# Stack ends: variance, mean and gates at other places in their engines' orders; entry: v weights and chunk 1 rounded between q and k

## The chip, the cores and the metric

The kernel runs on one core of a Trainium2 chip. That core has TensorE (PE, matrix products; PEld is its weight load), VectorE (DVE), ScalarE (ACT), GpSimd (POOL) and SyncE (SP, which issues the DMAs). Every engine works through its own list of instructions in the order in which they were written, and the engines meet only through semaphores. The metric is the device time of one execution in microseconds. The kernel before took 3382.31 us (median of 3 runs, 3380.04 to 3384.08).

## The reference

The input is 2048 tokens of width 128. Two stacks (the same weights, different input) stand around a Mamba block:

```python
x = x + 0.5 * ffn_ref(layernorm(x))        # stack 0: DEPTH = 6 layers
x = x + mamba_ref(layernorm(x))
x = x + 0.5 * ffn_ref(layernorm(x))        # stack 1: the same six layers

for i in range(6):                         # inside ffn_ref
    x = attn_layer(shift_tokens(x), ...) + x   # q,k,v = x @ Wqkv, l2norm, rotary,
                                               # windows of 32 keys, softmax, @ Wo
    x = ffn_layer(shift_tokens(x), ...) + x    # layernorm (mean, variance), W1, a*gelu(gate), W2
```

## The kernel before, in words

The tokens lie along the free axis, 16 tiles of 128 tokens per layer, 96 tiles per stack. A tile goes through a software pipeline whose steps `s` are counted up to 114: at every step each engine does its own piece of tiles of different age, in the order in which the step functions are called in `tensor_stack`, `scalar_stack`, `vector_stack` and `pool_stack`. There is no scheduler: the order written in these functions is the order on the engines.

**Entry of a stack.** The input is normalised in four chunks of 512 tokens (`square_in`, `rsqrt_in`, `scale_in`). Products of q, k and v are made from a high and a low part: ACT rounds weights (`high_weights`, L805) and input chunks (`high_input`, L794) to the high part, POOL subtracts to get the low part (`low_weights`, L1544; `low_input`, L1535). After `q_project(0)` and `k_project(0)` the first tile's chain is: ACT squares q and k (`q_square` L832, `k_square` L839), DVE rotates (`q_rotate1` L1190, `q_rotate2` L1199, `k_rotate1` L1208, `k_rotate2` L1214), sums squares (L1226, L1232) and floors the sums (`floor_sums`, L1238), POOL adds the halves (`q_add_halves` L1562, `k_add_halves` L1568) and multiplies with the inverse norms (`q_normalise` L1576, `k_normalise` L1584; the inverse norms are ACT L850). q's and k's second rotated halves share one buffer, T2, so `q_rotate2(1)` waits until POOL has done `k_add_halves(0)`, and `k_project(1)` on PE waits for `q_rotate2(1)`. In stack 1 POOL also clears PTS (`memset` L1623), which `p_evacuate(0)` on ACT needs later.

**End of a stack.** The feed-forward part works on units of four tiles. The last four tiles are two units of 256 columns, which the code calls `u + 1` (tiles 92 and 93) and `u + 2` (tiles 94 and 95), with `u` the last unit of 512. The end is written out by hand (`finish_tiles` on PE, the code behind the step loop on the others). A unit goes: mean product (`centre_product`, L427), square (ACT L932), variance product (L447), inverse root (`inverse_root`, ACT L942 and L944), normalise (DVE L1284, L1286), high part (ACT L957), low part (POOL L1596), up products (L468 to L470, 18 matmuls), gelu (ACT L971), gate (DVE L1308, three), down products (`down_products`, L521, three matmuls, which the trace shows as six), and `half_output` (DVE L1329, L1331), which adds the result to X. `residual(95)` on DVE (L1270, L1271) must be done before the mean product of `u + 2`, and it follows `out_products(95)` on PE (L404), which follows `o_evacuate(95)` on ACT (L922) and `value_products(95)` on PE (L384). The Mamba block starts when the last `half_output` is done; at the end of stack 1 the same event lets SP send the last piece of the output.

Of the kernel before, what the change touches and what calls it, by code (L numbers as in the profile page):

```python
# [31 lines left out]
def build(nc, xT, consts, wqkv, wo, w1, w2, lpar, qks, mpar, in_w, xp_w, dt_w, out_w, out):  # L32
    ctx = ExitStack()
    with ctx:
# [61 lines left out]
        PTS = take(2048)  # L96
# [95 lines left out]
        def tensor_stack(pe, r):  # L192
# [352 lines left out]
            def finish_tiles():  # L545
# [6 lines left out]
                u = UNITS - 3  # L552
# [42 lines left out]
                centre_product(u + 1, 4)  # L595
                tile(oT_ev, 94)
                out_products(94, 2)
                tile(PT_ev, 95)
                pe.wait_ge(v2_in[1], 160 * ((n0 + 95) // 2 + 1))
                value_products(95)  # L600
                units(f_sq, u + 1)
                variance_product(u + 1, 5)
                tile(oT_ev, 95)
                tile(res_done, 94)
                out_products(95, 2)
                units(f_lo, u + 1)
                up_products(u + 1, 0, 0)
                up_products(u + 1, 1, 1)
                units(f_done, u)
                up_products(u + 1, 2, 3)  # L610
                tile(res_done, 95)
                units(f_xm, u + 1)
                centre_product(u + 2, 4)
                units(f_sq, u + 2)
                units(f_ln, u + 1)
                variance_product(u + 2, 5)
# [150 lines left out]
        def scalar_stack(act, r):  # L767
# [66 lines left out]
            def k_square(n):  # L834
                if not 0 <= n < N:
                    return
                act.wait_ge(k_done, n0 + n + 1)
                act.wait_ge(q_ss, n0 + n + 1)
                act.activation(SQ, PS[:, 0, :], ACT.Square).then_inc(k_sq, 1)  # L839
# [166 lines left out]
            for s in range(114):  # L1006
                if s == 17 + 1:
                    square_in(3)
                    high_weights(0, 2)
                    high_input(1)  # L1010
                if s == 17 + 2:
                    rsqrt_in(3)
                    high_input(2)
                    if r == 0:
                        act.wait_ge(const_in, 48)
                if s == 19 + 2:
                    split_up(0)
                if s == 19 + 4:
                    high_input(3)
                ffn_high(s - 23)  # L1020
                split_k(s - 18)
                exponentials(s - 20)
                q_evacuate(s - 19)
                o_evacuate(s - 21)
                k_evacuate(s - 19)
                gelu0(s - 23)
                gelu1(s - 23)
                gelu2(s - 23)
                q_square(s - 17)
                v_evacuate(s - 19)  # L1030
                restore_tables(s - 23)
                inverse_norms(s - 18)
                carry_evacuate(s - 18)
                split_input(s - 24)
                ffn_square(s - 22)
                ffn_rsqrt(s - 22)
                p_evacuate(s - 20)
                k_square(s - 17)
                split_v(s - 19)
                split_q(s - 17)  # L1040
# [13 lines left out]
            p_evacuate(95, 0)  # L1054
            tables(act)
            square(u + 1, 4)
            o_evacuate(95)
            inverse_root(u + 1, 5)
            high_part(u + 1)
            square(u + 2, 4)  # L1060
            inverse_root(u + 2, 5)
# [101 lines left out]
        def vector_stack(dve, r):  # L1163
# [257 lines left out]
            gate(u + 1, 0, 0)  # L1421
            gate(u + 1, 1, 1)
            gate(u + 1, 2, 3)
            half_output(u + 1, 5)
            gate(u + 2, 0, 6)
            gate(u + 2, 1, 7)
            gate(u + 2, 2, 2)
            half_output(u + 2, 4)

        def vector_mamba(dve):  # L1430
# [98 lines left out]
        def pool_stack(pool, r):  # L1529
# [85 lines left out]
            for s in range(113):  # L1615
                if s == 17 + 1:
                    low_weights(0, 2)
                    low_input(1)
                if s == 17 + 2:
                    low_input(2)  # L1620
                    if r == 1:
                        pool.wait_ge(m_out, 4)
                        nc.gpsimd.memset(PTS, 0.0).then_inc(zero_set, 1)  # L1623
                if s == 17 + 8:
                    low_input(3)
                ffn_low(s - 23)
# [254 lines left out]
```

## Time and profile before

| | us |
|---|---|
| median of 3 runs | 3382.31 |
| lowest, highest | 3380.04, 3384.08 |
| the profiled execution | 3384.22 |
| its span, first to last instruction | 3382.3 |
| PE busy | 3193.0 (94%) |
| DVE busy | 2792.2 (83%) |
| ACT busy | 2509.8 (74%) |
| POOL busy | 2434.0 (72%) |
| mean granted TensorE clock | 0.984 |

The profiled execution took 1.9 us more than its span. Stack 0 runs from the start to 1548.85 us, the Mamba block from there to about 1835 us, and stack 1 to the end. In the slices of the page PE is at 9 tenths in nearly all of both stacks, and lower in the first slice and in the Mamba block, so the change touches four short stretches at whose edges PE isn't full: two entries and two ends.

### The profile page before, as it was taken

How to read it: one execution, taken by the hardware profiler on the slowest of the kernel's cores; microseconds unless marked ns; L12 is line 12 of the kernel's file. 1: busy time of each engine (PE TensorE's matmuls, PEld its weight loads, DVE VectorE, ACT ScalarE, POOL GpSimd, SP SyncE). 2: the span in 40 equal slices, each digit the busy share in tenths (PEclk: the TensorE clock that was granted, in tenths of full speed). 3: DMA queues.
4: the chain of work that ended last, by engine and by line, in shares of the span. 5: the costliest groups of instructions: out<-in, count | busy, mean ns of one | idle time of the engine just before them, and what ended most of it. 6: DMA issues, size and time to landing. Idle time of an engine off the chain costs nothing.

```text
span 3382.3 us, 120360 instructions
## 1 busy us (share of the span) xinstructions
PE 3193.0 (94%) x51584; PEld 2524.8 (75%) x51584; DVE 2792.2 (83%) x3200; ACT 2509.8 (74%) x3167; POOL 2434.0 (72%) x1227
## 2 busy tenths in 40 slices
PE   7999999999999999997788899999999999999998
PEld 5888887887888887773223788888878788888776
DVE  6888888888888888875897888888888888888885
ACT  5777777777787777776675677777777777777775
POOL 6777776776777777750998777777768768768663
PEclk9999999999999999998899899999999999999999
DMA  3333233233333332221000332323323323323222
GB/s 112 89 76 89 69 89 84 69 85 83 77 78 91 73 83 66 72 70 37 10 1 0 83 77 69 91 69 82 91 67 87 90 70 79 94 64 90 64 65 64
DMA packets 142298, 245.21 MB, mean 72 GB/s; under 512 B 32397, under 2 KB 34638, under 8 KB 141774
## 3 DMA queue, kind: packets, MB, share of 16 engines
q1 hardware_dynamic: 141774, 237.51, 27.6%
q8 instruction: 415, 6.80, 0.8%
q14 instruction: 109, 0.89, 0.1%
HBM read 35.01 MB, written 1.05 MB: 11 GB/s over the span
## 4 chain that ended last, share of the span: by engine, by line
PE 78%; DVE 7%; issue 7%; POOL 4%; ACT 4%; DMA 0%; DVEq 0%; SPq 0%; POOLq 0%; ACTq 0%
PE PS L264 14%; PE PS L384 11%; PE PS L208 8%; PE PS L404 8%; PE PS L210 7%; PE PS L209 7%; PE PS L325 6%; PE PS L521 4%; ACT ARENA L860 3%; PE PS L468 2%; PE PS L470 2%; PE PS L469 2%; POOL ARENA L1672 2%; PE PS L427 1%; DVE ARENA L1496 1%
## 5 line engine op out<-in xcount | busy, mean ns | idle before, releaser
L1576 POOL TENSOR_TENSOR ARENA<-ARENA,RN 128x1024 f32<-128x1024 f32 x192 | 365.4, 1903 | 454.9 <-ACT RN L850 454.9
L264 PE MATMUL PS<-C,ARENA 128*128 128x128 f32 x4608 | 613.9, 276 | 33.3 <-ACT ARENA L860 16.3
L1568 POOL TENSOR_TENSOR ARENA<-ARENA 128x1024 f32<-128x1024 f32 x192 | 468.4, 2439 | 232.9 <-DVE ARENA L1214 231.9
L264 PEld LDWEIGHTS PS<-C,ARENA 128*128 128x128 f32 x4608 | 512.3, 141 | 110.2 <-issue 76.9
L208 PE MATMUL PS<-WL,XH 128*128 128x512 f32 x1152 | 490.1, 425 | 19.1 <-DVE ARENA L1214 7.4
L913 ACT ACTIVATE ARENA<-PS 64x1024 f32<-64x1024 f32 x384 | 390.2, 1016 | 98.5 <-PE PS L264 95.0
L1562 POOL TENSOR_TENSOR ARENA<-ARENA 128x1024 f32<-128x1024 f32 x192 | 457.4, 2382 | 4.2 <-DVE ARENA L1199 4.2
L210 PE MATMUL PS<-WH,XH 128*128 128x512 f32 x1152 | 455.9, 396 | 0.0
L209 PE MATMUL PS<-WH,XL 128*128 128x512 f32 x1152 | 454.3, 394 | 0.0
L384 PE MATMUL PS<-ARENA 128*64 128x64 f32 x12288 | 403.2, 224 | 41.8 <-DVE ARENA L1252 26.0
L384 PEld LDWEIGHTS PS<-ARENA 128*64 128x64 f32 x12288 | 378.3, 139 | 76.5 <-issue 76.3
L1190 DVE TENSOR_TENSOR ARENA<-PS,TAB 128x1024 f32<-128x1024 f32 x192 | 235.1, 1225 | 229.9 <-ACT ARENA L832 229.8
L1590 POOL TENSOR_TENSOR ARENA<-ARENA,RI 128x1024 f32<-128x1024 f32 x192 | 365.8, 1905 | 47.7 <-DVE RI L1263 41.4
L404 PEld LDWEIGHTS PS<-ARENA 128*128 128x128 f32 x3072 | 372.1, 191 | 18.0 <-ACT ARENA L922 1.8
L1584 POOL TENSOR_TENSOR ARENA<-ARENA,RN 128x1024 f32<-128x1024 f32 x192 | 374.5, 1950 | 1.5 <-ACT RN L850 1.5
L404 PE MATMUL PS<-ARENA 128*128 128x128 f32 x3072 | 373.9, 275 | 1.0 <-ACT ARENA L922 1.0
L325 PEld LDWEIGHTS PS<-ARENA 64*32 64x32 f32 x24576 | 292.4, 105 | 69.5 <-issue 59.2
L325 PE MATMUL PS<-ARENA 64*32 64x64 f32 x24576 | 326.0, 223 | 0.3 <-issue 0.3
L1244 DVE TENSOR_REDUCE MX<-PS 128x16 f32<-128x1024 f32 x192 | 234.5, 1222 | 94.6 <-PE PS L325 91.7
L922 ACT ACTIVATE ARENA<-PS 128x1024 f32<-128x1024 f32 x192 | 196.9, 1026 | 143.4 <-PE PS L384 143.4
L208 PEld LDWEIGHTS PS<-WL,XH 128*128 128x128 f32 x1152 | 218.5, 190 | 77.1 <-issue 17.6
L832 ACT ACTIVATE ARENA<-PS 128x1024 f32<-128x1024 f32 x192 | 197.1, 1027 | 98.4 <-PE PS L210 98.4
(147 smaller groups left out, 6487.7 us busy)
## 6 DMA issues: line engine op xcount, KB each, us to landing
ARENA<-ARENA SPq DMA_DIRECT2D x1152, 128.0 KB
ARENA<-ARENA SPq DMA_DIRECT2D x768, 64.0 KB
ARENA<-in_wqkv SPq DMA_DIRECT2D x36, 512.0 KB, 5.1
ARENA<-in_wo SPq DMA_DIRECT2D x12, 512.0 KB, 4.0
ARENA<-in_w SPq DMA_DIRECT2D x12, 341.0 KB, 3.6
ARENA<-in_w SPq DMA_DIRECT2D x12, 192.0 KB, 4.1
X<-in_xT SPq DMA_DIRECT2D x4, 256.0 KB, 5.7
out<-X SPq DMA_DIRECT2D x1, 768.0 KB, 3.4
```

Source lines behind the costliest of these rows:

```text
L208: nc.tensor.matmul(o, XH[:, x], WL[:, s], start=True, stop=False)
L209: nc.tensor.matmul(o, XL[:, x], WH[:, s], start=False, stop=False)
L210: last = nc.tensor.matmul(o, XH[:, x], WH[:, s], start=False, stop=True)
L264: last = nc.tensor.transpose(PS[:, slot, 128 * j:128 * j + 128], src[:, 128 * j:128 * j + 128], ident)
L325: last = nc.tensor.matmul(PS[32 * win:32 * win + 32, slot, c:c + 64], q[a:b, hp, 32 * win:32 * win + 32], kt[a:b, hp, 32 * win:32 * win + ...
L384: last = nc.tensor.matmul(out.rearrange("p (a q) -> p a q", a=2)[:, :, col:col + 32], v2[:, win, hp, :], pt[:, hp, win, :], start=True, st ...
L404: last = nc.tensor.matmul(PSB[:, bank, 0:128], w[:, 128 * j:128 * j + 128], OTS[:, 128 * j:128 * j + 128], start=j == 0, stop=j == 7)
L913: last = act.activation(blocks[a:b, :, par, :], PS[a:b, slot, :].rearrange("p (b q) -> p b q", q=32), ACT.Copy)
L1562: nc.gpsimd.tensor_tensor(QN[n % 2], QN[n % 2], T2, ALU.add).then_inc(q_add, 1)
L1568: nc.gpsimd.tensor_tensor(KN[n % 2], KN[n % 2], T2, ALU.add).then_inc(k_add, 1)
L1584: nc.gpsimd.tensor_tensor(a, a, bc(RN[:, n % 2, 16:32], 64), ALU.mult).then_inc(k_nrm, 1)
L1590: nc.gpsimd.tensor_tensor(heads(P), heads(P), bc(RI[:, n % 2, :], 64), ALU.mult).then_inc(p_nrm, 1)
```

## The change

No instruction is added or taken away. These move:

- PE, both stack ends: the variance product of `u + 1` goes ahead of `value_products(95)`; the mean product of `u + 2` goes up between the first and the second of the three up products of `u + 1`.
- ACT, both stack ends: `inverse_root(u + 1)` goes ahead of `o_evacuate(95)`.
- DVE, both stack ends: `half_output(u + 1)` goes behind the three gates of `u + 2`.
- ACT, both entries: the high parts of the v weights and of input chunk 1 go from behind `square_in(3)` to ahead of `k_square(0)`.
- POOL, both entries: `low_input(2)` goes from step 19 to step 22, and in stack 1 the clearing of PTS from step 19 to step 20.

```diff
@@ finish_tiles (PE)
                 out_products(94, 2)
+                units(f_sq, u + 1)
+                variance_product(u + 1, 5)
                 tile(PT_ev, 95)
                 pe.wait_ge(v2_in[1], 160 * ((n0 + 95) // 2 + 1))
                 value_products(95)
-                units(f_sq, u + 1)
-                variance_product(u + 1, 5)
                 tile(oT_ev, 95)
                 tile(res_done, 94)
                 out_products(95, 2)
                 units(f_lo, u + 1)
                 up_products(u + 1, 0, 0)
+                tile(res_done, 95)
+                units(f_xm, u + 1)
+                centre_product(u + 2, 4)
                 up_products(u + 1, 1, 1)
                 units(f_done, u)
                 up_products(u + 1, 2, 3)
-                tile(res_done, 95)
-                units(f_xm, u + 1)
-                centre_product(u + 2, 4)
@@ k_square (ACT)
+                if n == 0:
+                    high_weights(0, 2)
+                    high_input(1)
@@ scalar_stack
                 if s == 17 + 1:
                     square_in(3)
-                    high_weights(0, 2)
-                    high_input(1)
@@
             square(u + 1, 4)
+            inverse_root(u + 1, 5)
             o_evacuate(95)
-            inverse_root(u + 1, 5)
@@ vector_stack
-            half_output(u + 1, 5)
             gate(u + 2, 0, 6)
             gate(u + 2, 1, 7)
             gate(u + 2, 2, 2)
+            half_output(u + 1, 5)
             half_output(u + 2, 4)
@@ pool_stack
-                if s == 17 + 2:
+                if s == 17 + 3 and r == 1:
+                    pool.wait_ge(m_out, 4)
+                    nc.gpsimd.memset(PTS, 0.0).then_inc(zero_set, 1)
+                if s == 17 + 5:
                     low_input(2)
-                    if r == 1:
-                        pool.wait_ge(m_out, 4)
-                        nc.gpsimd.memset(PTS, 0.0).then_inc(zero_set, 1)
```

The end of a stack on PE, as the difference of the two orders: L404 is `out_products`, L384 `value_products(95)`, L447 the variance product of `u + 1`, L427 a mean product.

```order
 L427 MATMUL PS<-ARENA,C 128x256
 L404 MATMUL PS<-ARENA 128x128 x8
-L384 MATMUL PS<-ARENA 64x2x32 x32
 L447 MATMUL PS<-ARENA,C 128x256
+L384 MATMUL PS<-ARENA 64x2x32 x32
 L404 MATMUL PS<-ARENA 128x128 x8
 L468 MATMUL PS<-XNH,W1L 128x256
```

The variance product is now one place further ahead, in front of the 32 value products. The mean product of `u + 2` moves up by twelve matmuls in the same way (the diff above shows it).

The end of stack 1 on DVE before: L1308 are the gates (three a unit), L1329 and L1331 the two halves of `half_output`.

```order
L1308 SCALAR_TENSOR_TENSOR ARENA<-PS,LP,ARENA 128x256 x2
L1308 SCALAR_TENSOR_TENSOR ARENA<-PS,LP,ARENA 85x256
L1329 SCALAR_TENSOR_TENSOR X<-PS,LP,X 64x256
L1331 SCALAR_TENSOR_TENSOR X<-PS,LP,X 64x256
L1308 SCALAR_TENSOR_TENSOR ARENA<-PS,LP,ARENA 128x256 x2
L1308 SCALAR_TENSOR_TENSOR ARENA<-PS,LP,ARENA 85x256
L1329 SCALAR_TENSOR_TENSOR X<-PS,LP,X 64x256
L1331 SCALAR_TENSOR_TENSOR X<-PS,LP,X 64x256
```

And now (in the changed kernel these lines have numbers that are higher by one):

```order
L1309 SCALAR_TENSOR_TENSOR ARENA<-PS,LP,ARENA 128x256 x2
L1309 SCALAR_TENSOR_TENSOR ARENA<-PS,LP,ARENA 85x256
L1309 SCALAR_TENSOR_TENSOR ARENA<-PS,LP,ARENA 128x256 x2
L1309 SCALAR_TENSOR_TENSOR ARENA<-PS,LP,ARENA 85x256
L1330 SCALAR_TENSOR_TENSOR X<-PS,LP,X 64x256
L1332 SCALAR_TENSOR_TENSOR X<-PS,LP,X 64x256
L1330 SCALAR_TENSOR_TENSOR X<-PS,LP,X 64x256
L1332 SCALAR_TENSOR_TENSOR X<-PS,LP,X 64x256
```

All six gates now stand ahead of both half outputs.

The entry of stack 1 on POOL before, from `low_input(1)` on: L1535 makes low parts of input chunks, L1568 is `k_add_halves`, L1576 `q_normalise`, L1562 `q_add_halves`, L1584 `k_normalise`, L1623 clears PTS, and in the piece after it L1591 (before L1590) is `p_normalise(0)`.

```order
L1535 TENSOR_TENSOR XL<-ARENA,XH 128x512
L1568 TENSOR_TENSOR ARENA<-ARENA 128x1024
L1576 TENSOR_TENSOR ARENA<-ARENA,RN 128x1024
L1562 TENSOR_TENSOR ARENA<-ARENA 128x1024
L1584 TENSOR_TENSOR ARENA<-ARENA,RN 128x1024
L1535 TENSOR_TENSOR XL<-ARENA,XH 128x512
L1623 MEMSET ARENA 128x2048
L1568 TENSOR_TENSOR ARENA<-ARENA 128x1024
L1576 TENSOR_TENSOR ARENA<-ARENA,RN 128x1024
L1562 TENSOR_TENSOR ARENA<-ARENA 128x1024
L1584 TENSOR_TENSOR ARENA<-ARENA,RN 128x1024
L1568 TENSOR_TENSOR ARENA<-ARENA 128x1024
```

And now:

```order
L1536 TENSOR_TENSOR XL<-ARENA,XH 128x512
L1569 TENSOR_TENSOR ARENA<-ARENA 128x1024
L1577 TENSOR_TENSOR ARENA<-ARENA,RN 128x1024
L1563 TENSOR_TENSOR ARENA<-ARENA 128x1024
L1585 TENSOR_TENSOR ARENA<-ARENA,RN 128x1024
L1569 TENSOR_TENSOR ARENA<-ARENA 128x1024
L1577 TENSOR_TENSOR ARENA<-ARENA,RN 128x1024
L1563 TENSOR_TENSOR ARENA<-ARENA 128x1024
L1585 TENSOR_TENSOR ARENA<-ARENA,RN 128x1024
L1622 MEMSET ARENA 128x2048
L1569 TENSOR_TENSOR ARENA<-ARENA 128x1024
L1591 TENSOR_TENSOR ARENA<-ARENA,RI 128x1024
```

`low_input(2)` is gone from this place (it now stands ahead of `k_add_halves(4)`), and the clearing of PTS now stands ahead of `k_add_halves(2)` and `p_normalise(0)`. The row ahead of this piece, the low part of the v weights, keeps its place on POOL, but ACT's part before it comes earlier.

## Rows read from the trace of the kernel before

**Rows 1.** The page's chain that ended last, share of the span by engine.

```profile
PE 78%; DVE 7%; issue 7%; POOL 4%; ACT 4%; DMA 0%; DVEq 0%; SPq 0%; POOLq 0%; ACTq 0%
```

**Rows 2.** Stretches: from:to us, length, busy of each engine, granted clock, DMA share, GB/s.

```profile
20.00:30.00 10.00, 7.87 (x25) 5.03 (x24) 7.23 (x9) 4.27 (x6) 3.92 (x3) 0.84 0.02 7
...
200.00:1480.00 1280.00, 1250.79 (x21810) 1032.29 (x21806) 1083.69 (x1246) 982.74 (x1212) 942.67 (x466) 1.00 0.31 78
...
1536.00:1542.00 6.00, 5.71 (x22) 5.35 (x23) 1.26 (x3) 4.32 (x8) 0.24 (x1) 0.50 0.00 0
```

**Rows 3.** Timeline, PE, end of stack 0: start, length, instruction, [idle before <-releaser].

```profile
1522.96 2.08 PE L384 MATMUL PS<-ARENA 128*64 128x64 f32 x64
...
1526.16 2.05 PE L404 MATMUL PS<-ARENA 128*128 128x128 f32 x16 [0.49 <-ACT ARENA L922]
1529.14 0.39 PE L468 MATMUL PS<-XNH,W1L 128*128 128x256 f32 x1 [0.92 <-POOL XNL L1596]
...
1532.42 0.70 PE L447 MATMUL PS<-ARENA,C 128*128 128x256 f32 x2 [0.47 <-ACT ARENA L932]
1536.29 0.58 PE L468 MATMUL PS<-XNH,W1L 128*128 128x256 f32 x1 [3.17 <-POOL XNL L1596]
...
1540.30 2.40 PE L521 MATMUL PS<-ARENA 128*128 128x256 f32 x6
1545.27 2.57 PE L521 MATMUL PS<-ARENA 128*128 128x256 f32 x6 [2.57 <-DVE ARENA L1308]
```

**Rows 4.** Timeline, ACT, end of stack 0.

```profile
1527.87 0.42 ACT L957 ACTIVATE XNH<-ARENA 128x256 fp32r<-128x256 f32 x1 [0.94 <-DVE ARENA L1286]
...
1540.54 0.47 ACT L971 ACTIVATE ARENA<-PS,LP 85x256 f32<-85x256 f32 x1 [0.81 <-PE PS L470]
```

**Rows 5.** Timeline, DVE, end of stack 0.

```profile
1528.55 0.29 DVE L1271 TENSOR_TENSOR ARENA<-PS,ARENA 64x128 f32<-64x128 f32 x1
...
1543.75 1.26 DVE L1308 SCALAR_TENSOR_TENSOR ARENA<-PS,LP,ARENA 128x256 f32<-128x256 f32 x3
```

**Rows 6.** Timeline, PE and DVE, end of stack 1.

```profile
3371.74 1.47 PE L521 MATMUL PS<-ARENA 128*128 128x256 f32 x6
...
3378.72 0.47 DVE L1329 SCALAR_TENSOR_TENSOR X<-PS,LP,X 64x256 f32<-64x256 f32 x1 [3.19 <-PE PS L521]
3379.20 0.49 DVE L1331 SCALAR_TENSOR_TENSOR X<-PS,LP,X 64x256 f32<-64x256 f32 x1
```

**Rows 7.** Timeline, DVE, PE and ACT, entry of stack 0.

```profile
33.66 1.23 DVE L1190 TENSOR_TENSOR ARENA<-PS,TAB 128x1024 f32<-128x1024 f32 x1 [0.57 <-ACT ARENA L832]
...
35.40 1.23 DVE L1199 TENSOR_TENSOR ARENA<-PS,TAB 128x1024 f32<-128x1024 f32 x1 [0.52 <-POOL ARENA L1568]
...
36.88 0.47 PE L208 MATMUL PS<-WL,XH 128*128 128x512 f32 x1 [1.30 <-DVE ARENA L1199]
...
38.55 1.02 ACT L839 ACTIVATE ARENA<-PS 128x1024 f32<-128x1024 f32 x1 [4.18 <-PE PS L210]
```

**Rows 8.** Timeline, all engines, entry of stack 1.

```profile
1857.30 2.00 POOL L1544 TENSOR_TENSOR WL<-ARENA,WH 128x1024 fp32r<-128x1024 f32 x1 [4.55 <-ACT WH L805]
...
1858.99 1.22 DVE L1190 TENSOR_TENSOR ARENA<-PS,TAB 128x1024 f32<-128x1024 f32 x1 [2.06 <-ACT ARENA L832]
...
1862.86 1.23 DVE L1199 TENSOR_TENSOR ARENA<-PS,TAB 128x1024 f32<-128x1024 f32 x1 [2.65 <-POOL ARENA L1568]
...
1864.34 0.76 PE L208 MATMUL PS<-WL,XH 128*128 128x512 f32 x1 [3.43 <-DVE ARENA L1199]
...
1867.28 1.02 ACT L839 ACTIVATE ARENA<-PS 128x1024 f32<-128x1024 f32 x1 [7.58 <-PE PS L210]
...
1884.72 2.37 POOL L1568 TENSOR_TENSOR ARENA<-ARENA 128x1024 f32<-128x1024 f32 x1
...
1892.42 1.06 PE L264 MATMUL PS<-C,ARENA 128*128 128x128 f32 x8 [0.16 <-issue]
```

**Rows 9.** One line's instructions, L1238: shortest/median/longest in ns.

```profile
L1238 DVE TENSOR_SCALAR SS<-SS x192: 115/118/2144, 31.8 to 3321.2; 128x32 f32<-128x32 f32 x192
```

## The prediction

> **What bounds the kernel now.** I read the chain that ended last first: 78% of the span is PE's [rows 1]. The table of stretches then says that in the loop PE is busy 1250.79 of 1280 us [rows 2], so nothing is to be had or lost there unless an order of the loop changes, and none does. What the change touches are the edges, so I read the timelines of the two entries and the two ends, engine by engine, and looked at the idle time in brackets. At the end of stack 0 PE waits 0.49 us for ACT, 0.92 for POOL, 0.47 for ACT, 3.17 for POOL and, between the two down products, 2.57 for the gates on DVE [rows 3]. At the entry of stack 1, DVE waits 2.65 us for POOL's `k_add_halves(0)` and PE 3.43 us behind it; at the entry of stack 0 the same two waits are 0.52 and 1.30 [rows 7, 8]. An edge is a single chain: each us taken out of its longest path moves everything after it, because what follows waits for it.
>
> **End of a stack, the gates.** Before, DVE stands in `half_output(u + 1)` until PE has done the down products of `u + 1`, and only then makes the three gates of `u + 2` (1543.75 to 1545.01 us) [rows 5], though the last gelu of `u + 2` was done at 1541.01 [rows 4]. PE's second down product waits for these gates [rows 3]. Now the gates come first: the last one starts at 1541.05 and takes about 0.42 (a third of 1.26), so it is done at 1541.5, while PE is in the first down product until 1542.70. The second follows at about 1542.6 instead of 1545.27: 2.7 us less. `half_output(u + 1)` now runs beside the second down product; nothing waits for it but X, and at the end of stack 1 its small output transfer. In stack 1 the first down product ran at the higher clock (1.47 us, 3371.74 to 3373.21) [rows 6]. With no gap the second should too: 3373.21 + 1.4 + 0.04 + the 0.97 us of `half_output` = 3375.6 instead of 3379.69 [rows 6], 4.1 us less. Bounds: if it takes 2.57 us as in stack 0, 2.9 us less; if stack 0's pair ran at the higher clock, 1.1 (2.57 - 1.47) to 2.0 us more there.
>
> **End of a stack, variance and mean.** In times of stack 0. The variance product of `u + 1` starts at 1522.96 ahead of the value products [rows 3] and pushes them by about 0.43 us (0.70 long, its tail lies under the next). So `out_products(95)` starts at 1526.6 instead of 1526.16: this is the price, since ACT's `o_evacuate(95)`, for which it waits, comes that much later. What it buys: ACT's inverse root and DVE's normalise now lie beside the value products. The high part, before at 1527.87 [rows 4], goes right behind `o_evacuate(95)` at about 1526.5, and POOL's low part (0.72 us) is done at 1527.7, before `out_products(95)` ends at 1528.6. The 0.92 us wait ahead of the up products is gone, and they start at 1528.45 instead of 1529.14. Then the mean product of `u + 2` stands behind the first third of them and needs `residual(95)`: `out_products(95)` ends at 1528.64, the residual takes 0.6 us (before it ended at 1528.84) [rows 5], so PE waits some 0.15 us. The 18 matmuls and the mean product took from 1529.14 to 1531.95 (1532.42 less the 0.47 idle) [rows 3], 2.81 us. ACT's square now lies beside the other twelve, so the 0.47 wait goes. New start of the last variance product: 1528.45 + 0.15 + 2.81 = 1531.4, less 0.1 for a shorter tail, 1531.3: 1.1 us less. The 3.17 us chain behind it (root, normalise, high, low) stays as it is. The bounds: 0 if the residual comes so late that PE waits out the gain (0.7 + 0.47 us), 1.3 if no wait is left. I take 1.1, for both stacks.
>
> **Entry of stack 1.** ACT is idle ahead of `k_square(0)`, so rounding the v weights (1.05 us) and chunk 1 (0.62) there costs nothing; ACT's next input, k's product, comes later. POOL then makes the low v weights right after `q_add_halves(0)`, near 1852.8 instead of 1857.30 [rows 8], and `k_add_halves(0)` starts near 1856 and ends near 1858.3. `q_rotate2(1)` no longer waits for it: it follows `q_rotate1(1)` [rows 8], and its 2.65 us of idle time go. What is late next is PE's own square of q, at which `q_rotate1(1)` already waits. So `k_project(1)` starts 2.65 us earlier, after an idle time of 0.8 us instead of 3.43. In stack 0 it ran after 1.30 us idle with 0.47 us for its first matmul, in stack 1 with 0.76; to the next square it took 1.67 us there (36.88 to 38.55) and 2.94 here (1864.34 to 1867.28) [rows 7, 8]. That is the two clocks, and I expect the higher one here now: another 1.27. Together 3.9 us. If the clock stays low it is 2.65.
>
> **Entry of stack 0.** The same wait is 0.52 us there [rows 7], so 0.5 less. The v weights must have landed by 23 us instead of 28.7: the DMA engines are at 0.02 from 20 to 30 us [rows 2], so they had.
>
> **What POOL moves elsewhere.** `low_input(2)` (1.3 us) goes ahead of `k_add_halves(4)`, where POOL is idle for about a us; its user is the q product of tile 8. Nothing. The clearing of PTS (1.8 us) goes ahead of `k_add_halves(2)`, which stands at 1884.72 with no idle time before it [rows 8], so it does delay that and `p_normalise(0)` by 1.8 us. The latter ended at 1888.95, and PE's transpose of it started at 1892.42 behind other work [rows 8]: 3.4 us of cover, so nothing. If that cover were gone it would cost up to 1.8 us.
>
> **A rule that could speak against it.** L1238, VectorE's floor of the sums, takes 118 ns in the median and 2144 at most [rows 9]; the long ones end when a POOL instruction beside them ends. The Trainium skill (SBUF — State Buffer, "Who interferes with whom") says why: VectorE in a two-port mode and GpSimd share a port pair, and the later one fully blocks. By that rule the earlier `k_add_halves(0)` now stands beside the floor in both entries and holds it to about 33.6 and 1858.3 us. Without the rule the floor ends 1.7 or 1.4 us earlier, at 31.9 and 1856.9. The next rotation starts at 33.66 and 1858.99 [rows 7, 8] either way, but in stack 0 the margin is 0.1 us, so the 0.5 there is the weakest term. I keep it and put the loss into a rival.
>
> **The sum.** 0.5 + (2.7 + 1.1) + 3.9 + (4.1 + 1.1) = 13.4 us. The profiled execution took 3384.2, which gives 3370.8; the median of the runs is 1.9 lower, which gives 3368.9, or 3369.
>
> **The rivals.**
>
> *The stack ends give the reordering back, and the clock stays low at stack 1's entry* (0.15). For it: `out_products(95)` is later and the mean product now waits on a later residual; the clock there was low once [rows 8]. Against: the waits of 0.92 and 0.47 us do go. It costs 2 x 1.1 + 1.3 = 3.5 us: 3372.5.
>
> *The clock does better* (0.12). In stack 0's end the rows show 0.50 from 1536 to 1542 us although PE was busy 5.71 of 6 us [rows 2]; down products took 2.40 and 2.57 [rows 3] against 1.47 in stack 1 [rows 6]. With the gap of 2.57 gone, both could run at the higher clock, as could the first products of the Mamba block: 0.9 + 1.1 + about 1.5: 3365.5. The Trainium skill (TensorE: Matmul & The Clock Gate, Part 1) has the clock released by activity and low without it; by that, continuous work favours this case. The stretch at 0.50 with PE nearly full speaks against taking it as the forecast.
>
> *POOL's moved work shows* (0.07). The clearing of PTS and the blocked floor decide: 1.8 + 0.5 us: 3371.3.
>
> *Only the ends count* (0.05). The loop that follows swallows what the entries gain, because something other than this chain (a transfer, POOL) sets when PE is full. Against: from tile 4 on PE has almost no idle time, so an earlier start stays. 4.4 us back: 3373.3.
>
> *The loop settles at a longer pitch* (0.03, the slower side). Engines wait for each other in a circle, and an entry with other offsets could leave one more short wait in each step. PE's 0.16 us wait ahead of a transpose shows the kind [rows 8]; one more of it in each of 192 tiles is 31 us, less 13: 3400. It decides from 13.4 / 192 = 0.07 us a tile on. Against: the order in the loop is the same, and both stacks, with different entries, take the same time for the loop within about 2 us.
>
> *Most of it doesn't work* (0.03): another wait stands at once behind each one removed, and less than half of the sum is left: 3377.
>
> The forecast has 0.55. Its own spread from the clock (1.3 us a term) and from runs that differ by 2 us is 3365.5 to 3372.5. The range that should hold 8 in 10 reaches up to the first rival and half of the fourth and down to the second: 3364 to 3374.5. What a measurement can tell here is about 0.2%, 6.8 us, so faster means under 3375.5: 0.92. Within it 0.05; slower 0.03.
>
> **What the profile after would show.** No wait of DVE for L1568 in either entry, and `k_project(1)` in stack 1 after an idle time of about 0.8 us, with matmuls of 0.4 us. In the ends: no idle time between the two down products, the six gates behind each other, the last variance product 1.1 us closer to `out_products(94)`. The loop between as long as before. The prediction is wrong if `q_rotate2(1)` still waits for POOL, if PE idles over 0.5 us ahead of the moved mean product, or if the stretch from tile 8 to tile 90 has another length.

## The result, and the profile after

The changed kernel took 3362.34 us (median of 4 runs, 3360.05 to 3367.87), the kernel before 3382.48 us beside it (4 runs). The ratio is 0.9943 with a 95% interval of 0.9926 to 0.9961: 20.1 us less, where 13.4 were forecast. The time lies below the range given. The profiled execution took 3364.21 us with a span of 3362.4, 20.0 us less than the profiled execution before (3384.22).

The end of stack 0 on PE, timeline of the changed kernel (start, length, instruction, idle time before it), answers to [rows 3]:

```profile
1523.44 1.95 PE L404 MATMUL PS<-ARENA 128*128 128x128 f32 x16
1525.22 0.60 PE L447 MATMUL PS<-ARENA,C 128*128 128x256 f32 x2
...
1528.96 2.05 PE L404 MATMUL PS<-ARENA 128*128 128x128 f32 x16 [1.12 <-ACT ARENA L925]
1530.77 0.37 PE L468 MATMUL PS<-XNH,W1L 128*128 128x256 f32 x1
...
1531.70 0.70 PE L427 MATMUL PS<-ARENA,C 128*128 128x256 f32 x2
...
1533.67 0.59 PE L447 MATMUL PS<-ARENA,C 128*128 128x256 f32 x2
1537.43 0.58 PE L468 MATMUL PS<-XNH,W1L 128*128 128x256 f32 x1 [3.17 <-POOL XNL L1597]
...
1541.16 2.97 PE L521 MATMUL PS<-ARENA 128*128 128x256 f32 x12
1545.20 3.70 PE L683 MATMUL PS<-X,C 128*128 128x512 f32 x8 [1.07 <-DVE X L1332]
```

The up products follow `out_products(95)` without idle time, the last variance product follows the up products without idle time, and the two pairs of down products are one group of 12 that takes 2.97 us; before they were 2.40, a gap of 2.57, and 2.57 [rows 3]. The same pieces before, not among the rows above, with the first products of the Mamba block as the last:

```profile
1521.08 1.95 PE L404 MATMUL PS<-ARENA 128*128 128x128 f32 x16
...
1548.91 5.44 PE L683 MATMUL PS<-X,C 128*128 128x512 f32 x8 [1.07 <-DVE X L1331]
```

The same eight products take 3.70 us now and took 5.44 then. The new order of the gates explains the gap that went. It can't explain this: the products are the same and nothing stands between them, so it is the clock. The stretches (from:to, length, busy of PE, PEld, DVE, ACT, POOL, granted clock, DMA share, GB/s) say so, first of before, then of after:

```profile
1545.00:1553.00 8.00, 6.66 (x12) 3.38 (x13) 4.18 (x8) 0.93 (x2) 0.00 (x0) 0.57 0.22 72
1863.00:1878.00 15.00, 11.64 (x123) 9.07 (x127) 11.52 (x10) 6.50 (x8) 11.22 (x6) 0.66 0.00 0
```

```profile
1538.00:1544.00 6.00, 6.00 (x30) 5.17 (x28) 3.65 (x8) 3.79 (x7) 0.00 (x0) 0.77 0.01 4
1541.00:1549.00 8.00, 6.93 (x24) 3.99 (x23) 6.01 (x11) 3.61 (x6) 0.00 (x0) 1.00 0.25 74
1851.00:1864.00 13.00, 9.04 (x103) 6.92 (x105) 10.59 (x10) 6.81 (x10) 8.54 (x4) 1.00 0.00 0
...
200.00:1480.00 1280.00, 1250.67 (x21855) 1032.59 (x21856) 1083.74 (x1248) 983.31 (x1211) 942.15 (x466) 1.00 0.31 78
```

Around the last down products the clock was 0.50 [rows 2] and is 0.77; at the start of the Mamba block it was 0.57 and is 1.00; at the entry of stack 1, 0.66 and 1.00. The loop is what it was: PE busy 1250.67 of 1280 us, against 1250.79. Summed over the span, the granted clock was at its lower level (1.2 of 2.4 GHz) for 106 us before and for 78 after (an expectation below has 108, which counts 2 us behind the last instruction).

DVE at the end of stack 0, and at the end of stack 1 with PE's down products, timelines of the changed kernel, answer to [rows 5, 6]:

```profile
1541.86 0.48 DVE L1309 SCALAR_TENSOR_TENSOR ARENA<-PS,LP,ARENA 85x256 f32<-85x256 f32 x1 [0.47 <-ACT ARENA L974]
1542.65 0.48 DVE L1330 SCALAR_TENSOR_TENSOR X<-PS,LP,X 64x256 f32<-64x256 f32 x1 [0.31 <-PE PS L521]
...
1544.17 0.48 DVE L1330 SCALAR_TENSOR_TENSOR X<-PS,LP,X 64x256 f32<-64x256 f32 x1 [0.53 <-PE PS L521]
```

```profile
3355.21 3.49 PE L521 MATMUL PS<-ARENA 128*128 128x256 f32 x12
...
3359.23 0.49 DVE L1332 SCALAR_TENSOR_TENSOR X<-PS,LP,X 64x256 f32<-64x256 f32 x1
```

The last gate now follows its gelu, and the half outputs wait for PE only. In stack 1, 4.5 us lie between the start of the down products and the end (3355.21 to 3359.72), against 7.95 before (3371.74 to 3379.69 [rows 6]).

The entry of stack 1, timeline of the changed kernel, DVE, PE, ACT and POOL, answers to [rows 8]:

```profile
1848.66 1.53 DVE L1239 TENSOR_SCALAR SS<-SS 128x32 f32<-128x32 f32 x1
...
1852.03 1.21 DVE L1200 TENSOR_TENSOR ARENA<-PS,TAB 128x1024 f32<-128x1024 f32 x1
```

```profile
1853.49 0.47 PE L208 MATMUL PS<-WL,XH 128*128 128x512 f32 x1 [0.69 <-DVE ARENA L1200]
...
1860.36 0.47 PE L208 MATMUL PS<-WL,XH 128*128 128x512 f32 x1 [1.65 <-DVE ARENA L1215]
...
1877.71 1.06 PE L264 MATMUL PS<-C,ARENA 128*128 128x128 f32 x8 [0.16 <-issue]
```

```profile
1855.15 1.02 ACT L842 ACTIVATE ARENA<-PS 128x1024 f32<-128x1024 f32 x1 [3.56 <-PE PS L210]
...
1844.59 1.99 POOL L1545 TENSOR_TENSOR WL<-ARENA,WH 128x1024 fp32r<-128x1024 f32 x1
...
1847.78 2.38 POOL L1569 TENSOR_TENSOR ARENA<-ARENA 128x1024 f32<-128x1024 f32 x1
```

`q_rotate2(1)` (L1200) waits for nobody, and `k_project(1)` comes after 0.69 us of idle time, not 3.43 [rows 8], with a first matmul of 0.47 us, not 0.76. The entry of stack 0, DVE and PE, answers to [rows 7]:

```profile
33.35 1.23 DVE L1191 TENSOR_TENSOR ARENA<-PS,TAB 128x1024 f32<-128x1024 f32 x1 [0.18 <-ACT ARENA L832]
34.49 1.21 DVE L1200 TENSOR_TENSOR ARENA<-PS,TAB 128x1024 f32<-128x1024 f32 x1
```

```profile
36.60 0.58 PE L208 MATMUL PS<-WL,XH 128*128 128x512 f32 x1
...
43.76 0.76 PE L208 MATMUL PS<-WL,XH 128*128 128x512 f32 x1 [2.58 <-DVE ARENA L1215]
```

DVE's wait of 0.52 us went here too. But `q_project(2)`, at 43.76, stands behind 2.58 us of idle time, and it and the first v product run at the lower clock through all their twelve matmuls: from tile 3 on stack 0 is 1.9 us *later* than before in this profile.

Set one beside the other, start by start, the two traces give this account. "Waits" is what the idle time that went brought to the next piece, "clock" is the same instructions taking another time.

| stretch | forecast | trace | waits | clock |
|---|---|---|---|---|
| entry of stack 0 | 0.5 | -1.9 | 0 | -1.9 |
| loop of stack 0 | 0 | -0.5 | | |
| end of stack 0 | 3.8 | 6.1 | 3.8 | 2.3 |
| Mamba block | 0 | 4.4 | 0 | 4.4 |
| entry of stack 1 | 3.9 | 6.0 | 2.7 | 3.3 |
| loop of stack 1 | 0 | 0.6 | | |
| end of stack 1 | 5.2 | 5.3 | 3.8 | 1.5 |
| sum | 13.4 | 20.0 | 10.3 | 9.6 |

The forecast of 13.4 had some clock in it already: 1.27 us in the entry of stack 1 and about 1.5 at the end of stack 1.

### The profile page after: what moved, and what is told of

Same layout as the page of the kernel before. It is cut to its first block, busy times and chain, and to the rows that moved or that the text cites. A ratio compares the mean times of both kernels' runs of the same rounds, so it can differ in the third digit from the quotient of the medians.

```text
span 3362.4 us, 120360 instructions
## 1 busy us (share of the span) xinstructions
PE 3178.5 (95%) x51584; PEld 2519.0 (75%) x51584; DVE 2793.3 (83%) x3200; ACT 2511.4 (75%) x3167; POOL 2434.8 (72%) x1227
## 4 chain that ended last, share of the span: by engine, by line
PE 77%; DVE 7%; issue 7%; POOL 5%; ACT 4%; DMA 0%; DVEq 0%; SPq 0%; POOLq 0%; ACTq 0%
PE PS L264 14%; PE PS L384 11%; PE PS L208 8%; PE PS L404 8%; PE PS L210 7%; PE PS L209 7%; PE PS L325 6%; PE PS L521 4%; ACT ARENA L863 3%; PE PS L468 2%; PE PS L470 2%; PE PS L469 2%; POOL ARENA L1673 2%; PE PS L427 1%; DVE ARENA L1497 1%
## 5 line engine op out<-in xcount | busy, mean ns | idle before, releaser
L384 PE MATMUL PS<-ARENA 128*64 128x64 f32 x12288 | 404.5, 225 | 41.7 <-DVE ARENA L1253 25.8
L384 PEld LDWEIGHTS PS<-ARENA 128*64 128x64 f32 x12288 | 379.5, 139 | 76.8 <-issue 76.8
L1591 POOL TENSOR_TENSOR ARENA<-ARENA,RI 128x1024 f32<-128x1024 f32 x192 | 366.0, 1906 | 47.2 <-DVE RI L1264 37.1
L404 PEld LDWEIGHTS PS<-ARENA 128*128 128x128 f32 x3072 | 372.1, 191 | 18.6 <-ACT ARENA L925 2.5
L404 PE MATMUL PS<-ARENA 128*128 128x128 f32 x3072 | 373.8, 275 | 2.2 <-ACT ARENA L925 2.2
```

What stands on the lines that cost most here:

```text
L384: last = nc.tensor.matmul(out.rearrange("p (a q) -> p a q", a=2)[:, :, col:col + 32], v2[:, win, hp, :], pt[:, hp, win, :], start=True, st ...
L404: last = nc.tensor.matmul(PSB[:, bank, 0:128], w[:, 128 * j:128 * j + 128], OTS[:, 128 * j:128 * j + 128], start=j == 0, stop=j == 7)
L1591: nc.gpsimd.tensor_tensor(heads(P), heads(P), bc(RI[:, n % 2, :], 64), ALU.mult).then_inc(p_nrm, 1)
```

## The experiments

The theory (T): the waits went as forecast, some 10.5 us in all, and the rest is TensorE's clock, which stays up where PE no longer stops. The rival (S): some part has a structural gain of its own that the forecast overlooked. A median of 11 runs has an interval of about 3 us on either side, one of 5 runs about 4 to 5, so no two results closer than that are told apart by the medians alone. The kernel before took 3382.3 to 3383.7 us beside these kernels.

### The parts, each alone

**Gates.** The kernel before with DVE's change alone (as in the diff of the change, `vector_stack`).

> The kernel before with the gates of the last unit ahead of half_output of the unit before it, in both ends, and nothing else. Theory T (the moves gain what their waits cost, and the rest of the gain of 20 us is TensorE's clock, which is granted at its low level for fewer us): 2.7 us in stack 0 and 4.1 in stack 1 by the waits, 6.8, and some us more where the last products and the first ones of the Mamba block get the high clock: 7 to 10 us less than before, and no stretch at the low clock behind the last up products longer than 3.4 us. Rival S (a structural gain was overlooked in one of the parts, the clock differs by chance): exactly one of the three part kernels gains 6 us more than its waits say; here that would be 13.

3374.98 us, ratio 0.9977 (0.9968 to 0.9986): 8.7 less. The timeline of PE at the end of stack 0 in this kernel:

```profile
1541.55 3.48 PE L521 MATMUL PS<-ARENA 128*128 128x256 f32 x12
1546.11 3.70 PE L683 MATMUL PS<-X,C 128*128 128x512 f32 x8 [1.07 <-DVE X L1331]
```

The gates alone join the down products and bring the Mamba block's first products to the higher clock (3.70 us). They are worth 4.0 us in stack 0's end by the trace, 2.57 of it the gap (the pair itself took 3.48 us instead of 4.97), and 1.7 in the first products behind it, which the Mamba block gave back later in this profile.

**Variance and mean.** The changes of `finish_tiles` on PE and of `inverse_root` on ACT alone.

> The kernel before with the variance product, the mean product and ACT's inverse root moved in both ends, and nothing else. Theory T: 1.1 us in each end, 2.2 less, plus or minus 2 by the clock. Rival S: 8 less. Rival G (the reorder is given back by the later out products): no gain.

3377.86 us, ratio 0.9984 (0.9975 to 0.9993): 5.8 less, against 2.2 forecast. That is outside T's 2.2 plus or minus 2 and under S's 8, and with an interval of 3 us it decides between neither. In its profile each end's waits give 1.2 to 1.3 us, as worked out; another 2.4 in the end of stack 0 and 1.4 in that of stack 1 come from matmuls that ran at the higher clock. The down products at the end of stack 0 in this kernel:

```profile
1540.26 1.47 PE L521 MATMUL PS<-ARENA 128*128 128x256 f32 x6
1544.30 1.54 PE L521 MATMUL PS<-ARENA 128*128 128x256 f32 x6 [2.57 <-DVE ARENA L1308]
```

The idle times of 3.17 and 2.57 us stand here as before, and still these products took 1.47 and 1.54 us, not 2.40 and 2.57 [rows 3]. So an idle time doesn't always slow the same work behind it. In the six profiles whose end of stack 1 is that of the kernel before (before, e_entry, entry_act_only, entry_pool_only, s0_entry, s1_entry) the stretch from the last variance product to the end took from 16.8 to 19.1 us with the same idle times. What holds in every profile is the first eight products of the Mamba block: 3.70 us in the nine profiles where the gap of 2.57 is gone or filled, 5.18 to 6.56 us in the seven where PE idles in it.

**Entry.** ACT's and POOL's changes of both entries.

> The kernel before with the entry's moves on ACT and POOL in both stacks, and nothing else. Theory T: 0.5 us in stack 0 and 2.65 in stack 1 by the waits, and 1.3 to 3 by the clock in stack 1: 4.5 to 6 less than before; in stack 0 the profile can show up to 2 us more than before, where the low clock falls on the products of tiles 2 and 3. Rival S: 10 less.

3374.92 us, ratio 0.9981 (0.9973 to 0.9990): 8.7 less, against 4.4 forecast; T had 4.5 to 6 and S 10, and the median is nearer to S. Its profile has 5.5 us in stack 1's entry.

**The whole again**, on the same chip as these three.

> The changed kernel once more, on the chip of its parts. Theory T: 20 us less than before, in single runs from 14 to 24, and the time falls with the total of us at the low clock (78 us in the first profile, 108 in the one of before); the parts' gains add to less than the whole, or to it, since each frees the clock for the next. If the parts add to 13.4 and the whole is 20, the parts act together, by the clock. Rival S: the parts add to 20 on this chip with equal clock totals.

3361.24 us (5 runs), ratio 0.9936 (0.9923 to 0.9950): 22.4 less. The three parts add up to 23.2. So no gain from their working together is to be seen, and each part alone gave 2 to 4 us more than its forecast (1.9, 3.6 and 4.3 us). No one part holds the 6 to 7 us by which the whole beat its forecast. Each of these three surpluses is near the interval of its median, so that none of them alone shows a cause.

### The entry taken apart, and the ends together

```
e_entry split by stack:  if n == 0 and r == 1 (s1_entry)   if n == 0 and r == 0 (s0_entry)
e_entry split by engine: ACT's rounding (entry_act_only)   POOL's two moves (entry_pool_only)
ends_both:               gates + variance and mean, entries as before
```

> The kernel before with ACT's part of the entry moved alone: POOL keeps the low part of chunk 2 and the clearing of PTS ahead of the second tile's k addition. Theory T: these two stand where POOL has idle time in stack 0; in stack 1 the clearing delays the second k addition by up to 1 us, beside other work: the same gain as the whole entry (8.7 us) within 1 us. Rival P (POOL's moves carry part of the gain): 3 us or more of it is missing.

> Kernel before with ACT's and POOL's entry changes in stack 1 alone. T (the waits go as predicted, and fewer stops of PE let its clock stay up): nearly all of the entry's gain is here, since the wait was 2.65 us in stack 1 and 0.52 in stack 0: 6.5 to 8.5 us less than before (the whole entry change gave 8.7), of which 2.65 to 4 from the waits and the rest by the clock at the products behind them. S (a structural gain that I overlooked, in stack 0's entry): at most 5 us less here.

> Kernel before with ACT's and POOL's entry changes in stack 0 alone. T: 0 to 2 us less than before, since the wait that goes is 0.52 us. S (the overlooked gain is in stack 0's entry): 3 us less or more.

> Kernel before with POOL's part of the entry change alone (the low part of chunk 2 and the clearing of PTS later; ACT's rounding stays where it was, so the v weights' low part still stands ahead of k's halves). T: the wait of 2.65 us stays, and the only gain is that of the work taken away ahead of k_add_halves(1) and its kin, the same 2.3 us by which the whole entry change beats ACT's part alone: 1 to 3 us less. P (POOL's part matters for the time of the whole in its own right, as a chain that was late by the 1.8 us of the clearing): 3 us less or more. N (it does nothing, and the 2.3 us between the two were noise): within 1 us.

> Kernel before with the changes of the ends alone: gates, variance and mean, both stacks. T: the two parts add up, 8.7 + 5.8 = 14.5, so 13 to 16 us less. C (the clock's share is one common pool, which each part takes for itself when it is alone): 10 to 12 us less, since the waits of the ends are 7.7 by the working and the clock's share (some 8 us in the whole) is then counted once.

| kernel | median us (runs) | ratio, 95% | less than before |
|---|---|---|---|
| entry_act_only | 3377.23 (11) | 0.9981 (0.9972 to 0.9990) | 6.4 |
| s1_entry | 3377.57 (11) | 0.9982 (0.9973 to 0.9991) | 5.4 |
| s0_entry | 3381.24 (11) | 0.9995 (0.9986 to 1.0004) | 1.7 |
| entry_pool_only | 3383.66 (11) | 1.0000 (0.9991 to 1.0009) | -0.7 |
| ends_both | 3369.50 (5) | 0.9959 (0.9945 to 0.9973) | 13.4 |

Most of the gain of the entry is that of ACT's rounding in stack 1. POOL's moves do nothing by themselves: entry_pool_only is rival N's case, and T's 1 to 3 us did not come. entry_act_only missed T too (the same gain within 1 us), by 2.3 us, which P's 3 us or more doesn't cover either. On these 2.3 us stood my expectation for entry_pool_only; they were noise or need ACT's part, and the medians don't tell. The profiles speak for noise of the clock: in entry_act_only the four idle products that the kernel before has itself ahead of `k_project(0)` (`keep_clock`, L215) took 3.78 us in stack 1, in e_entry 1.99. s0_entry's 1.7 lies in T's 0 to 2, within its interval of nothing. s1_entry missed T's 6.5 to 8.5 by a us and is above S's bound of 5; with an interval of 3 us it decides nothing by its median. Its profile does: from tile 0 to tile 6 of stack 1 it gains 6.6 us where the waits are 2.7. The ends add up within the intervals (13.4 against 8.7 + 5.8), where a pool of clock shared by the parts would have given 10 to 12.

### The clock by itself: fillers

If the surplus is the clock's, it must be had without moving any real work, by giving PE idle products to do where it waits. These are matmuls into a bank that is free there, whose result nobody reads. The kernel before has some of the kind itself, ahead of `k_project(0)`, `q_project(1)` and `k_project(1)` (`keep_clock`); these are added:

```diff
+            def fill(k, bank):
+                for _ in range(k):
+                    nc.tensor.matmul(PSB[:, bank, 0:256], centre, C[:, 0:256], start=True, stop=True)
@@ finish_tiles: ahead of the last up products, and (before only) between the down products
+                fill(11, 6)
                 units(f_lo, u + 2)
                 up_products(u + 2, 0, 6)
...
+                fill(9, 0)
                 for j in range(3):
                     units(f_h[j], u + 2)
@@ entries: 4 and 10 such products ahead of the transposes of k of tiles 0 and 1, 4 ahead of q_project(2);
@@ in stack 1, before only: 10 ahead of k_project(1)
```

> The kernel before with extra products into free PSUM banks, whose results nobody reads, where PE idles: 11 ahead of the last unit's up products and 9 between the down products (both ends), 4 ahead of the first k transpose, 10 ahead of the second, 4 ahead of the third q product, and 10 ahead of the second k product of stack 1. No order of the real work is changed. Theory T (part of the change's gain is the clock): with the clock held, up and down products of the ends and the first Mamba products run at the high level: 8 us less than before. Rival S (waits alone): the same time as before, or some us more where a filler stands in the way.

> The changed kernel with the same extra products (without the 9 between the down products and the 10 ahead of the second k product, where it has no idle time left). Theory T: 3 to 5 us less than the changed kernel; and the distance to the filled kernel before is what the waits alone give, about 15 us, against 22 unfilled. Rival S: the distance stays 22.

> The changed kernel with the 11 extra products ahead of the last unit's up products in both ends alone. Theory T: 2 to 3 us less than the changed kernel: the up products of the last unit at the high clock (2.2 us for 18 instead of 3 to 4). Rival S: no gain.

before_filled took 3377.18 us (11 runs), 6.5 less than before; full_filled 3362.84 and full_filled_ends 3360.64 (5 runs each), against 3361.24 for the changed kernel (measured on another chip; the kernel before took 3383.65 and 3383.63 us on the two). The distance between the filled kernels is 14.3 us, near T's 15 and not S's 22. But T's 3 to 5 us, and 2 to 3 for the ends alone, did not come, before_filled had 6.5 of T's 8, and the waits give 10.3 and not 14.3. The profile shows why. PE in before_filled, end of stack 0:

```profile
1537.61 0.47 PE L482 MATMUL PS<-XNH,W1L 128*128 128x256 f32 x1
...
1539.91 1.46 PE L535 MATMUL PS<-ARENA 128*128 128x256 f32 x6
1541.20 4.05 PE L219 MATMUL PS<-C 128*128 128x256 f32 x18
1545.09 1.46 PE L535 MATMUL PS<-ARENA 128*128 128x256 f32 x6
```

The down products (L535) run at the higher clock, 1.46 us against 2.40 and 2.57 [rows 3]. But the fillers (L219; one of them shows as two) take 4.05 us where 2.57 were idle, so that 3.7 us lie between the down products, and there is no idle time ahead of the real products behind them: the fillers ended last, and took back what they gave. So I sized them to the idle time: 7, 5 (before only), and 5 in the place of each 10.

```diff
-                fill(11, 6)
+                fill(7, 6)
...
-                fill(9, 0)
+                fill(5, 0)
```

> Kernel before with fillers of a fitting length: 7 idle products ahead of the last up products of each stack end (3.2 us by the 4.91 us that 11 took in before_filled, for an idle time of 3.17), 5 between the two down products (2.2 us for 2.57), and 5 in place of 10 in the entries. No wait of the real work is changed, only what PE does in it. In before_filled PE had no idle time ahead of these products and the fillers ended last, so part of what the clock gave was taken back. T (the part of the gain that the waits don't explain, 9 to 12 us, is the clock's, and comes when PE merely keeps busy): 8 to 12 us less than before, against 6.5 with the longer fillers. S (the rest is structural, in the order of real work): not more than the 6.5 again, or less.

> The changed kernel with the same shorter fillers (7 ahead of the last up products, 4/5/4 in the entries). T: 1 to 3 us less than the changed kernel (3361.2), and 10 to 12 us less than before_filled_less, the sum of the waits that the change took out by the trace (3.8 + 2.8 + 3.8 = 10.4), as the clock is up in both. S: the distance between the two filled kernels stays 14 us or more.

| kernel | median us (runs) | ratio, 95% | less than before | time at the lower clock |
|---|---|---|---|---|
| before_filled | 3377.18 (11) | 0.9980 (0.9971 to 0.9989) | 6.5 | 77 |
| before_filled_less | 3370.68 (6) | 0.9967 (0.9955 to 0.9979) | 11.6 | 52 |
| full_filled | 3362.84 (5) | 0.9936 (0.9923 to 0.9948) | 20.8 | 52 |
| full_filled_ends | 3360.64 (5) | 0.9931 (0.9919 to 0.9944) | 23.0 | 65 |
| full_filled_less | 3356.81 (5) | 0.9930 (0.9917 to 0.9942) | 25.5 | 65 |

The last column is of the profiled run, in us. before_filled_less is the run that decides: the kernel before, in its old order, with idle products in PE's waits, is 11.6 us faster (by the interval of the ratio 7 to 15); S had at most 6.5 there. The step from the longer fillers, 5 us, is within the intervals by the medians; the two traces show it: from the last variance product to the end of the stack it is 15.1 and 17.7 us with the longer fillers, 13.1 and 15.7 with the shorter, in stack 0 and 1 (16.5 and 18.2 without any). PE at the end of stack 0 in before_filled_less:

```profile
1536.09 1.53 PE L535 MATMUL PS<-ARENA 128*128 128x256 f32 x6
1537.46 2.32 PE L219 MATMUL PS<-C 128*128 128x256 f32 x10
1540.20 1.53 PE L535 MATMUL PS<-ARENA 128*128 128x256 f32 x6 [0.41 <-DVE ARENA L1324]
1542.81 3.70 PE L699 MATMUL PS<-X,C 128*128 128x512 f32 x8 [1.07 <-DVE X L1347]
```

Between the starts of the two down products lie 4.1 us, with the gates still behind `half_output(u + 1)`; before they were 4.97 [rows 3]. The end of the first and the start of the second are 2.57 us apart, as before. The Mamba block's first products take 3.70 us. The stretch that was at 0.50 before [rows 2]:

```profile
1536.00:1542.00 6.00, 5.23 (x22) 4.01 (x22) 2.46 (x6) 1.75 (x2) 0.00 (x0) 1.00 0.01 1
```

full_filled_less has the lowest median of the study, 4.4 us below that of the changed kernel, where T had 1 to 3; the ratios of the two (0.9930 and 0.9936) overlap, so the medians don't show that it is faster. It stands 13.9 us from before_filled_less, T having 10 to 12 and S 14 or more: between the two, it speaks for neither. Piece by piece the two traces stand 4.1 (end of stack 0), 1.7 (entry of stack 1) and 4.0 us (end of stack 1) apart, 9.8 together, near the 10.4 of T's working; the rest of the 13.9 lies within the intervals of two ratios of 6 and 5 runs. PE in full_filled_less, end of stack 0:

```profile
1530.76 3.18 PE L219 MATMUL PS<-C 128*128 128x256 f32 x14
1534.10 0.39 PE L480 MATMUL PS<-XNH,W1L 128*128 128x256 f32 x1
...
1536.58 2.83 PE L533 MATMUL PS<-ARENA 128*128 128x256 f32 x12
```

The up products start 3.77 us after the variance product (1530.33), as in the changed kernel (1533.67 to 1537.43), and take 2.5 us where they took 3.7. From the last variance product to the end it is 1.4 us less than in the changed kernel at the end of stack 0 and 1.3 less in stack 1.

## Why the prediction was wrong

The direction and the mechanism of every wait were right; the step that failed is the one on the clock. By the traces the 6.6 us between 13.4 and 20.0 are 2.3 at the end of stack 0, 4.4 in the Mamba block, 2.1 in the entry of stack 1 and 0.2 at the end of stack 1 and in the loops, less the 2.4 by which the entry of stack 0 fell short. But for the 0.5 us of wait that did not arrive in the entry of stack 0, nearly all of it is clock. The largest of these pieces, the Mamba block's, is 1.7 us of cause and 2.7 us of luck, as said below.

**Gates, stack 0 (2.7 less).** The second down product follows the first without idle time, and `half_output(u + 1)` lies beside it. The gap of 2.57 went. I had named the bound "if stack 0's pair ran at the higher clock, 1.1 to 2.0 us more there", and it came: 2.97 us for both pairs instead of 4.97. From the first down product to the Mamba block it is 4.04 us instead of 8.61, 4.6 less.

**Gates, stack 1 (4.1 less).** 3.4 by the trace (2.57 of it the gap). The second pair did not run at the higher clock throughout (3.49 us for the two, where the forecast had 2.9); in exchange the up products before it did for the first half, and gave 0.65.

**Variance and mean (1.1 less, twice).** 11.34 us from `out_products(94)` to the last variance product before (1521.08 to 1532.42), 10.23 after (1523.44 to 1533.67): 1.11. In stack 1, 1.13. The price was as worked out: `out_products(95)` starts 0.44 us later against `out_products(94)`, with an idle time of 1.12.

**Entry of stack 1 (2.65 and 1.27 less).** 2.75 and 1.28 by the two traces. (The square at which `q_rotate1(1)` waits is ACT's; the prediction calls it PE's own.) What the forecast left out comes behind that: `q_project(2)` and the first v product, twelve matmuls from 1872.48 to 1877.0 before, take from 1860.36 to 1863.3 now, 1.6 us less, and the transposes of tile 1's k another 0.7. Both are clock, and s1_entry gains as much at this place (6.6 us).

**Entry of stack 0 (0.5 less), called the weakest term.** In this profile nothing of the wait arrived at `k_project(1)`: it is 0.28 us earlier than before, and `q_project(1)` ahead of it (30.62 against 30.94) already was 0.32 earlier. The four idle products between them (L215) took 2.34 us at the lower clock, 1.89 before, and PE went from them to `k_project(1)` without idle time. In full_again, where they took 1.89, the term came: 5.36 us from `q_project(1)` to `k_project(1)` against 5.94, 0.6 less. The clock took 1.9 us of this profile's entry; in full_again the entry is 1.5 us faster than before, in s0_entry and e_entry 0.7 faster and 0.8 slower. Kernels whose entry of stack 0 was unchanged scatter as widely, from 1.0 us faster (ends_both) to 1.0 slower (v_variance). Over the whole entry the term is not seen in this scatter.

**What POOL moves (nothing).** Right: entry_pool_only is 0.7 us from before. PE's transposes at 1877.71 keep their 0.16 us of idle time, though the clearing of PTS stands ahead of `p_normalise(0)` now.

**VectorE's floor.** L1239 took 1.53 us in the entry of stack 1 and 1.64 in that of stack 0, against 118 ns in the median [rows 9], and ended when POOL's `k_add_halves(0)` did. This is what the Trainium skill (SBUF — State Buffer, "Who interferes with whom") has, and the trace agrees. The rotation behind it waited for ACT in both entries, so it cost nothing.

**Failed: "The stretch at 0.50 with PE nearly full speaks against taking it as the forecast".** I saw that PE was busy 5.71 of 6 us at a clock of 0.50, concluded that the clock there does not answer to PE's idle time, and priced it as given, but for `k_project(1)` in stack 1's entry and the second down product of stack 1. The rows say otherwise when one looks at what PE did *before* the clock fell: 3.17 us of idle time ahead of that stretch, 2.57 ahead of the next one (which covered the Mamba block's first products), 3.43 ahead of the one in stack 1's entry. Where the gap of 2.57 was taken away, by real work or by idle products, the Mamba block's first products ran at the higher clock, in nine profiles of nine; where it stayed, in none of seven. Over the products between the two idle times the tie is looser, as v_variance shows. The busy share inside a low stretch doesn't speak for or against idle time as its cause: the up products there start 0.21 us apart and at the higher clock 0.12, so PE looks busy because its work takes longer.

The rival "The clock does better" had this mechanism, a chance of 0.12 and 3365.5 us. It named the down products and the Mamba block's first products, and these came with 2.0 and 1.7 us. It missed the entry (2.0 us more) and the Mamba block further on, where two low stretches of before, at 1678.7 and 1791.4, are absent in the profile after (2.7 us). That last piece is not dependable: full_again has both stretches and gains nothing there. The Trainium skill (TensorE: Matmul & The Clock Gate, Part 1) has the clock released by activity and low without it. The fillers agree: 106 us of low clock became 52, and 11.6 us went, without a wait of the real work being touched. I had cited that rule and given it a small chance for want of a second row.

**How much is the clock's stays a range.** By the two traces 9.6 of 20.0 us. The medians give 22.4 for the second set of runs, and 10.9 of waits (the 10.3 and the 0.6 that arrived in full_again) leave 11.5. Among the runs of the kernel before, the time falls by about 1.3 us per 0.001 of mean granted clock; the changed kernel has 0.989 against 0.984, which makes about 6. The distance between the filled kernels, 14, leaves 8. Each is rough; between 6 and 12 us, with the waits at 10 to 14.

## What to carry to other kernels

Where PE waits two or three microseconds on a chain, price two things: the wait, and the work behind it that ran at the lower clock on its account, the next block's too; here the second was about as large as the first by the traces. To see whether a low stretch belongs to a wait, look at PE's idle time ahead of it, and not at how busy PE was in it; and take more than one profile, since the same idle times were followed by slow products in one and by fast ones in another. Idle products in the wait put it to the test without moving real work, if they are a bit shorter than the idle time: with fillers that overran it, 2 us were lost at each stack's end.

## What the runs showed that I had not expected

The changed kernel still has 3.17 us of idle time in each end, and filling it (full_filled_less) gains 1.3 to 1.4 us in each by the trace. A kernel whose PE is busy for 94% of its span and whose mean granted clock is 0.984 had 11.6 us in the clock at its four edges and in what stands behind them. And the granted clock varies from run to run of one kernel: 0.982 in runs of the kernel before that took 3384 to 3385 us, 0.986 to 0.987 in runs that took 3376 to 3381.
